# Joining two DMA accumulators of attention probabilities before TensorE sums them

## The reference

```python
x = x + 0.5 * ffn(layernorm(x))          # sign weights, 512 -> 2048 -> 512, relu
x = x + attn(layernorm(x))
x = x + 0.5 * ffn(layernorm(x))
# attn: 16 heads of 32 features, 2 sequences
scores = einsum('bhqd,bhkd->bhqk', q, k) * SCALE
probs = softmax(scores, axis=-1)
attn = einsum('bhqk,bhkd->bhqd', probs, v)
```

## Time and profile before

| | |
|---|---|
| median of the runs | 3118.62 us (3116.81 to 3118.83) |
| the profiled execution | 3113.91 us, span 3112.0 us |
| busy share of the span | PE 96%, DVE 65%, ACT 52%, POOL 43% |
| mean granted TensorE clock | 0.986 of full speed |
| attention stage | about 926 to 2542 us from the first sums |

### The profile page before, as it was taken

One profiled execution on the slowest core, in us unless ns is written; L12 is line 12 of the kernel. 1 busy time (PEld: TensorE's weight loads), 2 busy tenths in 40 slices (PEclk: granted clock), 3 DMA queues, 4 the chain that ended last, 5 costly groups with the idle time before them and its releaser, 6 DMA issues.

```text
span 3112.0 us, 38839 instructions
## 1 busy us (share of the span) xinstructions
PE 2973.2 (96%) x14768; PEld 1964.9 (63%) x14768; DVE 2038.0 (65%) x3044; ACT 1613.9 (52%) x2851; POOL 1331.3 (43%) x489
## 2 busy tenths in 40 slices
PE   6999999998799999999999999999999889999998
PEld 4888887876555555555555555555555447888887
DVE  4555556766587777777787777787877234555552
ACT  5344443322166666666666666666666553333333
POOL 0000000000078787878787878788888700000000
PEclk9999999999899999999999999999999989999999
DMA  4110012563287888888888787878787754222200
GB/s 141 62 55 28 28 55 88 186 214 119 84 203 170 192 179 195 177 192 177 190 177 193 174 197 172 200 173 197 178 194 181 192 148 120 57 55 54 55 28 28
DMA packets 184891, 428.54 MB, mean 138 GB/s; under 512 B 89728, under 2 KB 90752, under 8 KB 148224
## 3 DMA queue, kind: packets, MB, share of 16 engines
q0 software_dynamic: 32400, 235.94, 32.7%
q1 hardware_dynamic: 152304, 190.11, 22.0%
HBM read 121.91 MB, written 67.63 MB: 61 GB/s over the span
## 4 chain that ended last, share of the span: by engine, by line
PE 71%; ACT 9%; DMA 6%; DVE 5%; POOL 4%; issue 4%; SPq 0%; ACTq 0%; POOLq 0%; DVEq 0%
PE bank L426 15%; PE bank L445 15%; PE bank L830 12%; PE bank L802 9%; PE bank L553 8%; ACT att_p L786 8%; PE bank L806 6%; DMA att_dma_acc<-att_p 5%; POOL att_acc L710 4%; PE bank L317 3%; DVE att_row_max L737 2%; PE bank L851 2%; PE bank L846 1%; DVE norm_inv L108 1%; ACT head_total L228 0%
## 5 line engine op out<-in xcount | busy, mean ns | idle before, releaser
L737 DVE TENSOR_REDUCE att_row_max<-bank 128x1 f32<-128x512 f32 x2048 | 1258.5, 683 | 383.5 <-PE bank L806 379.9
L786 ACT ACTIVATE att_p<-bank 128x512 f32<-128x512 f32 x2048 | 1047.0, 620 | 585.2 <-PE bank L802 573.2
L710 POOL TENSOR_TENSOR att_acc<-att_acc,att_p 128x2048 f32<-128x2048 f32 x217 | 993.4, 4578 | 222.9 <-ACT att_p L786 218.4
L802 PE MATMUL bank<-att_q,att_k 98*128 98x512 f32 x2048 | 852.7, 418 | 30.2 <-ACT att_p L786 25.6
L806 PE MATMUL bank<-att_k,att_q 96*128 96x512 f32 x2048 | 815.9, 400 | 48.8 <-DVE att_row_max L737 38.0
L802 PEld LDWEIGHTS bank<-att_q,att_k 98*128 98x128 f32 x2048 | 385.9, 189 | 403.1 <-issue 210.2
L830 PE MATMUL bank<-att_p,att_v 128*32 128x512 f32 x4096 | 502.1, 608 | 0.0
L806 PEld LDWEIGHTS bank<-att_k,att_q 96*128 96x128 f32 x2048 | 390.5, 191 | 123.6 <-DVE att_row_max L737 45.3
L369 DVE TENSOR_TENSOR ffn_hid_lo<-ffn_hid,ffn_hid_hi 128x512 fp32r<-128x512 f32 x256 | 176.1, 688 | 430.7 <-ACT ffn_hid_hi L404 412.8
L401 ACT ACTIVATE ffn_hid<-bank,up_s 128x512 f32<-128x512 f32 x256 | 176.1, 688 | 474.8 <-PE bank L426 474.2
L426 PE MATMUL bank<-hi,ffn_up_w 128*128 128x512 f32 x1024 | 402.7, 393 | 20.3 <-DVE lo L122 15.3
(11 more groups left out here) (89 smaller groups left out, 2215.9 us busy)
## 6 DMA issues: line engine op xcount, KB each, us to landing
att_dma_acc<-att_p POOLq DMA_DIRECT2D x225, 1024.0 KB, 7.6
x<-x_after_ffn SPq DMA_DIRECT2D x16, 1024.0 KB, 7.4
att_q<-q_hi SPq DMA_DIRECT2D x64, 256.0 KB, 4.2
att_k<-k_hi SPq DMA_DIRECT2D x64, 256.0 KB, 8.9
x<-xT SPq DMA_DIRECT2D x8, 1024.0 KB, 7.1
x_after_ffn<-x_out SPq DMA_DIRECT2D x8, 1024.0 KB, 9.3
q_hi<-qkv_o_hi SPq DMA_DIRECT2D x32, 256.0 KB, 2.0
q_lo<-qkv_o_lo SPq DMA_DIRECT2D x32, 256.0 KB, 2.5
```

Of the source, the lines that this page charges most:

```text
L710: self.nc.gpsimd.tensor_tensor(self.acc[H % 2][:], a[:], self.prob[kt % PR][:], ALU.add).then_inc(self.summed, 1)
L737: self.nc.vector.tensor_reduce(self.row_max[odd][:, qt, q:q + 1], m[:], axis=AX.X, op=ALU.max).then_inc(self.m_read, 1)
L786: self.nc.scalar.activation(self.prob[kt % PR][:, q * CH:(q + 1) * CH], self.s_ps[S_BANK[kt * QC + q]][:], ACT.Exp, scale=SCALE).then_inc( ...
L802: self.nc.tensor.matmul(self.s_ps[S_BANK[i]][:], self.k_st[H % NB][0:KM, kt * P:(kt + 1) * P], self.q_st[H % NB][0:KM, q * CH:(q + 1) * CH ...
```

## The change

The second DMA accumulator of a head is added to the first by one more accumulating DMA. GpSimd issues it at the start of the next head's key tiles (`join_chains`), after it has waited for both chains. TensorE then multiplies two accumulators by ones instead of three. This holds for all heads but the last, which has its sums as before.

The sums stand one group later (SUMS_AFTER = 3). ScalarE copies them before the first exponential of tile 8 rather than after the second of tile 6. VectorE inverts them after tile 14 rather than 12, and SP issues the rows of maxima before the inverse's store rather than after.

```diff
-SUMS_AFTER = 2
+SUMS_AFTER = 3
...
+    def join_chains(self, pool, H):
+
+        for x in range(CHAINS):
+            pool.wait_ge(self.dma_summed[x], 16 * all_moves(H, x))
+        if H > 0:
+            pool.wait_ge(self.chains_joined, 16 * H)
+        first, second = self.dma_acc[H % 2]
+        pool.sem_inc(self.move_begun, 1)
+        self.nc.gpsimd.dma_start(first[:], second[:], accum_op=ALU.add).then_inc(self.chains_joined, 16)
...
-        if H > 0 and kt == 12:
+        if H > 0 and kt == 14:
             self.head_out.invert(dve, H - 1)
...
     def scalar_tile(self, act, H, kt):
         self.tile_free(act, H, kt)
+        if H > 0 and kt == G * (SUMS_AFTER + 1):
+            act.wait_ge(self.t_ready, H)
+            self.head_out.copy_sums(act, H - 1, self.sums_bank(H - 1))
...
-            if q == 1 and H > 0:
-                if kt == G:
-                    act.wait_ge(self.p_used, KT * H)
-                    self.head_out.copy_out(act, H - 1, self.o_ps)
-                if kt == G * (SUMS_AFTER + 1):
-                    act.wait_ge(self.t_ready, H)
-                    self.head_out.copy_sums(act, H - 1, self.sums_bank(H - 1))
+            if q == 1 and H > 0 and kt == G:
+                act.wait_ge(self.p_used, KT * H)
+                self.head_out.copy_out(act, H - 1, self.o_ps)
...
     def sums(self, pe, H):
-        out, first = self.sums_bank(H), not direct(H)
+        out, first, last = self.sums_bank(H), not direct(H), H == NH - 1
...
-        for x in range(CHAINS):
-            pe.wait_ge(self.dma_summed[x], 16 * all_moves(H, x))
+        for x in range(CHAINS if last else 1):
+            if last:
+                pe.wait_ge(self.dma_summed[x], 16 * all_moves(H, x))
+            else:
+                pe.wait_ge(self.chains_joined, 16 * (H + 1))
...
                         head_out.move_sums(sp, H - 1)
-                        head_out.store_inverse(sp, H - 1)
                     if H < LAST:
                         att.max_rows(sp, H + 1)
+                    if H > 0:
+                        head_out.store_inverse(sp, H - 1)
...
                     for kt in range(KT):
+                        if H > 0 and kt == 0:
+                            att.join_chains(pool, H - 1)
                         att.pool_tile(pool, H, kt)
```

More of the change, by code:

```diff
@@ L663, in __init__ @@
         self.summed, self.dma_summed = c.sem("att_summed"), [c.sem(f"att_dma_summed{x}") for x in range(CHAINS)]
+        self.chains_joined, self.joined = c.sem("att_chains_joined"), c.sem("att_joined")
         self.move_begun, self.t_ready = c.sem("att_move_begun"), c.sem("att_t_ready")
@@ L851, in sums @@
                 ins = self.nc.tensor.matmul(out[rows, :], self.ones_sum[:], self.dma_acc[H % 2][x][:, q * CH:(q + 1) * CH],
-                                            start=False, stop=(x == CHAINS - 1))
+                                            start=False, stop=(x == CHAINS - 1 or not last))
         ins.then_inc(self.t_ready, 1)
```

## The result

The changed kernel takes 3077.24 us (median of 4 runs, 3072.22 to 3079.45), the one before 3118.66 us in the same comparison. The ratio is 0.9866, with a 95% interval of 0.9849 to 0.9883: 1.34% or 41.4 us faster. The profiled execution took 3079.45 us with a span of 3077.4 us, so its span is 34.6 us shorter than the one before. Some of it lies ahead of the attention, which begins 2.6 us later than before here (first score at 864.2 us against 861.6), in stages that the edit doesn't touch.

What follows compares the result with a forecast made beforehand. TensorE was taken to bound the attention stage. 30 x (0.86 + 0.5 + 0.15) = 45.3 us, less 1.5 for the last head, is 43.8; 3118.6 - 43.8 gives 3075 us, range 3066 to 3092.

Steps and rivals of the forecast that it cites:

- TensorE sets the pace: Attention stage: TensorE is busy 1523.89 of 1560.60 us and sets the pace, a head taking 51.28 us.
- Four products fewer, 0.86 us: TensorE's sums: one accumulator less removes eight records, saving 0.86 us in each head with sums in front of it.
- The copy ahead, 0.5 us: ScalarE's copy before the exponentials removes TensorE's wait at L806: gain 0.5 us per head, ends 0.2 and 0.61.
- The inverse, 0.15 us: VectorE's reciprocal moved to tile 14 lets TensorE's transpose of the maxima start earlier: gain 0.15 us, ends 0 and 0.3.
- The join is hidden: Join to sums is 17.6 us against a longest landing of 11.9; its 0.87 us issue is covered: cost nothing.
- The DMA engines: Join adds 5.2 us, giving 46.2 us of DMA work per head in some 49.8: cost nothing below 10.3 per join.
- The last head, a pause of 3.14 us: TensorE waits for VectorE's norm steps ahead of the mean's product: cost once 1.5 us, ends 0 and 5.
- The sum: Heads 1 to 30 gain 45.3 us, less 1.5: 43.8 us off the 3118.6 median.
- only the products are saved: Rival, chance 0.11: the copy delays the exponentials by 0.49 us, TensorE waits as much at a score; 3090 us.
- The rival of the late join: Chance 0.03: the join needs 19 us instead of 17.6, TensorE waits 1.4 us per head; 3117 us, no change.

Runs made afterwards that it cites:

- the later group: The changed kernel run once more beside two further variants, against 3115.11 us for the kernel before: 3074.63 us, ratio 0.9872.
- the first experiment: The kernel before with only the second accumulator joined to the first by a DMA; sums, copy and inverse stay in place: 3091.87 us, ratio 0.9933.
- two further copies: The changed kernel with GpSimd also copying the second accumulator to memory twice per head behind the join, 1 MB each: 3145.42 us, ratio 1.0104.
- the early sums: The changed kernel with, in the last head alone, the previous head's sums after group 2 again and copied ahead of tile 6: 3070.60 us, ratio 0.9861.
- the third experiment: The changed kernel with ScalarE's copy of the sums behind the second exponential of tile 8 instead of ahead of the first: 3091.31 us, ratio 0.9928.
- the first extra megabyte: The changed kernel with GpSimd also copying the second accumulator to memory once per head behind the join: 3085.82 us, ratio 0.9911.

## Why the prediction was right

I forecast 3075 us within 3066 to 3092; it is 3077.24, or 3074.63 in the later group. Point by point:

- *TensorE sets the pace.* Yes: 0.86 us off its stream shortened every head by 0.86 (the join alone: 51.27 to 50.41).
- *Four products fewer, 0.86 us.* L856 to L864 is 0.86 us, and 16 records are left.
- *The copy ahead, 0.5 us.* The pair with the sums lost 8.98 - 7.62 = 1.36 = 0.86 + 0.50. Undone by itself it costs 0.49.
- *The inverse, 0.15 us.* 0.10 us. From the product before it to the transpose it is 0.42 us now (1751.87 to 1752.29) and was 0.53, so the wait that I read as 0.3 us is under 0.2, as forecast; by the trace's sum of waits, which counts the weight load, it went from 0.51 to 0.41 us per head. Somewhat over-sized, within its ends.
- *The join is hidden.* Yes for TensorE. Its issue takes 0.88 us and is covered as said. But the margin was drawn with the old landings: I compared 17.6 us with a longest landing of 11.9. The distance from issue to sums is 1784.12 - 1766.37 = 17.75 us, and the join's own landings are 12.0 us in the median and 14.2 at most, so 3.5 us are left where I saw nearly 6. The longest landing of all, 17.3 us, is that of a copy behind the join, and TensorE doesn't wait for it. A group earlier the distance is about 12, and the first experiment shows the join late there by a little, in 21 heads.
- *The DMA engines.* 45.8 us of work in a head, where I had 46.2; my 5.2 us for the join is what its queue shows, the sum over all queues grew by 4.3. The reason that I gave for 5.2 was not good: the shortest landing of 5.1 us is a plain copy's (L722), no accumulation before landed in less than 6.8. That the engines are not the bound held; with two further copies the head is late behind landings, with GpSimd's own list full beside them. The copies from tile 1 on landed 4 us later in the median (9.2 to 13.2) where I had up to 5. GpSimd's waits for them were mis-sized: 1 to 2 us at moves 5 and 9 were forecast, and it is 82.7 us in 18 waits, up to 5.3 us each, all behind the first copies and so at moves 5 and 7. Nobody waits for GpSimd there, as argued. Overlooked was the other transfer in the crowd, the rows of maxima, for which TensorE begins to wait. The Trainium skill (page "DMA: Bandwidth & Descriptors", section "Bandwidth") gives 6.15 us of busy time for a load of 1 MB from HBM; both readings of the join, which touches no HBM, are less. The page's figure is for another kind of transfer, and here the measurement decides.
- *The last head, a pause of 3.14 us.* It is 3.32 us, and removing it gives back about as much (3.35 by one trace of each). The net of 1.5 us was too small a price in the profiled executions. From the sums that stand in head 30 to the next stage it took 2507.32 - 2382.33 = 124.99 us, at a granted clock of 0.85, and 122.44 in the later one at 0.86. Before, from the same place (2416.83 + 8.98 = 2425.81) to 2542.34, it was 116.53 at 0.88. The sums in head 30, which this stretch holds only after the change, the pause, and the shorter sums and earlier copy in the last head explain 1.7 + 3.3 - 1.4 = 3.6 of the 8.5 or 5.9 us. The rest is about what the clock took: an estimate by the granted clocks is 0.15 x 124.99 = 18.7 and 0.14 x 122.44 = 17.1 us lost, against 0.12 x 116.53 = 14.0 before, so 4.7 and 3.1 us for a rest of 4.9 and 2.3. My terms held it only in the upper price of 5 us. With the early sums, without the pause, the stretch is at 0.87; whether the pause lowers the clock or it differs by itself stays open, since two executions of one kernel had 0.85 and 0.86.
- *The sum.* 29 heads from 934.68 to 2382.33 take 1447.65 us, before 1490.64 (926.19 to 2416.83): 43.0 us against the 43.8 (29 x 1.51) of my terms. Ahead of them, from the first score to the first sums and counted to the same place (926.19 + 8.98 before), 3.1 us are gained, of which my terms have 1.5. Less the tail's 8.5 or 5.9 us that is 37.6 or some 40 us in the attention, for 43.8 forecast, and 41.4 and 40.5 by the medians of the whole. So the forecast of 3075 us is right by its terms, and its nearness to 3077.24 in part by luck: the early part gave more than was reckoned, the tail took more, and whole runs scatter by more than the difference.

Of the rivals, the one that only the products are saved, at 3090 us, has the time that the third experiment measures (3091.31), but there the copy stands behind the second exponential. Copied ahead, TensorE waited for it no more than 0.1 us, so that rival described a kernel that places the copy badly, not this one. The rival of the late join rested on two accumulations never having run at once; they had, since moves went out every 5.8 us and landed after 7.4 us in the median.

## What to carry to other kernels

When an engine in a tight row of work must also do an odd job, put the job where the engine waits for its first input anyway: here the same copy costs 0.1 us ahead of eight exponentials and 0.5 us after the second, and it holds for both copies. Work moved from the engine that sets the pace to one that doesn't gave its full length back here (0.86 us), but the margin of what is moved must be reckoned with the landings that the move itself brings (14.2 us at most for the join), not with those of the trace before (11.9). And it must be reckoned for every transfer in the crowd: the first to be felt by TensorE was not the join but the rows of maxima. Look, too, at every pair of a regular rhythm that is longer than the plain one: two bank waits of 0.4 us, which this edit left alone, were worth more than the inverse, the last head and one copy together.

## What the runs showed that I had not expected

The join changed the landings of all moves, not only of those close behind it. The moves' median went from 7.6 to 8.9 us and the longest from 11.9 to 17.3, at a DMA share that rose only from 0.80 to 0.92. And the price near the limit is not linear: the first extra megabyte cost a head 0.3 us (share 0.95), the second 1.4 us in the median (share 0.98).

GpSimd's adds look longer where an issue of a DMA stands right ahead of them: 4.57 us alone, 4.8 to 5.3 us at 0.9 to 1.6 us of issue that overlap with it. They are not: from the start of such an add to the next issue it is 4.54 us (1734.55 to 1739.09), and 4.53 where it stands alone (1769.21 to 1773.74). The two records together are what GpSimd spends per pair, so a mean of either misleads.
